# Per-group key, query and probability tiles, and an earlier start of the expert phase, in a fused attention and mixture-of-experts kernel

## The reference, cut to what matters

```
x = x + xattn(layernorm(x), ctx)        # 8 batches, S = 512, D = 256, 16 heads of 16
x = x + moe(layernorm(x))               # 8 experts, HID = 512, the top 2 of each token

xattn: q, k, v projections (k, v from ctx); softmax(q k^T / 4) v; output projection
moe:   gates from softmax(x Wg / 5), top 2, normalised;
       y = sum over the 2 chosen experts e of gate * (gelu(x W1[e] + b1[e]) W2[e] + b2[e])
```

## Time and profile before

| | us |
|---|---|
| time before, median of 3 runs | 816.91 |
| lowest and highest | 812.75, 820.35 |
| the profiled execution, own time | 811.37 |
| its span in the profile | 809.6 |
| last attention product (`pv`) begins | 528.91 |
| first output of the expert phase (`output(0)`) begins | 546.04 |

### The profile page before, as it was taken

How to read it: one execution, slowest core, us unless ns; L and a number is a source line. 1 busy time by engine, 2 the same in 40 slices (tenths; PEclk the granted TensorE clock), 3 DMA queues, 4 the chain that set the end, 5 groups by cost and what they waited for, 6 DMA issues and landing times.

```text
span 809.6 us, 16188 instructions
## 1 busy us (share of the span) xinstructions
PE 751.9 (93%) x4634; PEld 449.7 (56%) x4634; DVE 612.4 (76%) x1123; ACT 455.7 (56%) x663; POOL 393.1 (49%) x354
## 2 busy tenths in 40 slices
PE   7689999999999999999999988759999989999995
PEld 3333434444444444444443433338999879998994
DVE  6586687788788788788788788536786887777674
ACT  1146766766766776776766756744345334444441
POOL 6406125628728728728725604243444455344444
PEclk9669999999999999999999999979999999999998
DMA  5765766757767767757757668874444555454441
GB/s 184 220 164 169 203 171 222 202 184 253 209 196 254 209 191 253 203 182 249 214 169 249 169 161 291 276 241 96 75 94 74 85 128 111 71 79 71 71 74 12
DMA packets 90667, 136.23 MB, mean 168 GB/s; under 512 B 15464, under 2 KB 49224, under 8 KB 90200
## 3 DMA queue, kind: packets, MB, share of 16 engines
q1 hardware_dynamic: 76456, 116.80, 48.0%
q0 software_dynamic: 13296, 17.09, 12.1%
q10 hardware_dynamic: 832, 1.31, 0.5%
HBM read 71.25 MB, written 64.04 MB: 167 GB/s over the span
## 4 chain that ended last, share of the span: by engine, by line
PE 66%; DMA 10%; DVE 10%; issue 5%; ACT 5%; POOL 2%; SPq 1%; POOLq 1%; DVEq 0%; ACTq 0%
PE ps_pv L1521 13%; PE ring L1508 9%; PE ring L1650 8%; PE ring L1668 8%; PE ring L1495 6%; DMA out<-y_sb,xs 6%; PE ps_x L1552 6%; DVE negm L1073 4%; PE ps_x L1570 4%; PE ps_x L1562 3%; ACT probs L1001 3%; PE ring L1659 2%; PE ps_x L1580 2%; PE ps_x L1539 1%; PE ps_pv L1641 1%
## 5 line engine op out<-in xcount | busy, mean ns | idle before, releaser
L1073 DVE TENSOR_REDUCE negm<-ring 128x2 f32<-128x1024 f32 x256 | 310.2, 1222 | 74.7 <-PE ring L1495 72.7
L1001 ACT ACTIVATE probs<-ring 128x1024 f32<-128x1024 f32 x256 | 260.4, 1023 | 91.1 <-PE ring L1508 90.1
L888 POOL DMA_INDIRECT out<-y_sb,xs x71 | 110.2, 1553 | 143.7 <-DMA out<-y_sb,xs 80.7
L1521 PE MATMUL ps_pv<-probs,v_aug 128*32 128x512 f32 x1024 | 139.0, 615 | 5.8 <-ACT probs L1001 5.8
L1508 PE MATMUL ring<-q_st,k_st 64*128 64x512 f32 x512 | 127.9, 499 | 7.0 <-DVE negm L1073 7.0
L1495 PE MATMUL ring<-k_st,q_st 64*128 64x512 f32 x512 | 110.5, 432 | 13.2 <-ACT probs L1001 4.9
L1508 PEld LDWEIGHTS ring<-q_st,k_st 64*128 64x128 f32 x512 | 48.5, 187 | 109.4 <-issue 76.9
L1035 ACT CAST xsT_hi<-ps_pv 128x256 fp32r<-128x256 f32 x71 | 26.4, 372 | 130.8 <-PE ps_pv L1641 130.8
L779 POOL DMA_INDIRECT xs_dram<-xg,rows x64 | 63.4, 991 | 52.7 <-DVEq L1241 32.1
L1668 PE MATMUL ring<-w_hi,hT_hi 128*128 x284 | 85.4, 301 | 0.1
L1668 PE MATMUL ring<-w_lo,hT_hi 128*128 x284 | 80.1, 282 | 0.0
(11 more groups left out here) (189 smaller groups left out, 1205.6 us busy)
## 6 DMA issues: line engine op xcount, KB each, us to landing
k_st<-k_dram SPq DMA_DIRECT2D x64, 192.0 KB
q_st<-q_dram SPq DMA_DIRECT2D x64, 192.0 KB
xs<-xs_dram SPq DMA_DIRECT2D x71, 132.5 KB, 2.4
k_dram<-qk_hi SPq DMA_DIRECT2D x32, 256.0 KB
q_dram<-qk_hi SPq DMA_DIRECT2D x32, 256.0 KB, 2.8
o_dram<-oT SPq DMA_DIRECT2D x32, 256.0 KB, 4.2
w_dram<-w_sb SPq DMA_DIRECT2D x12, 512.0 KB, 4.2
w_hi<-w_dram SPq DMA_DIRECT2D x11, 512.0 KB, 7.3
```

What stands on the lines that cost most here:

```text
L888: pool.indirect_dma_start(out=out, out_offset=bass.IndirectOffsetOnAxis(ap=xs[j % AHEAD][:, TOKEN:TOKEN + 1].bitcast(I32), axis=0), in_=y_ ...
L1001: nc.scalar.activation(probs[:, kt, 2 * jp:2 * jp + 2, :], ring[PLACE["ST", u, p] % RINGS][:], ACT.Exp).then_inc(exp_done, 1)
L1073: nc.vector.tensor_reduce(negm[:, v % 2, :, jp, kt], ring[PLACE["MX", v, p] % RINGS][:], AX.X, ALU.max, negate=True).then_inc(max_free, 1)
L1521: mm = nc.tensor.matmul(ps_pv[2 * DH * j:2 * DH * (j + 1), :], v_aug[:, kt, HPG * g + j, :], probs[:, kt, j, :], start=(kt == 0), stop=(kt ...
```

## The change

What it does:

- `k_st` and `q_st` become four tiles `kq[g]`, one a group, with keys and queries side by side, and `probs` four tiles, one a key tile. They are laid out in an order (kq0, kq1, kq3, probs1, probs0, kq2, probs2, probs3) so that late weights can be loaded over each as it dies. The memsets and the ones rows become four pieces.
- SP's late loads are moved. Into the second and third group of body 7 come `load_b2` (from behind `fetch_o(7, 0)`) and both `load_b1` (from behind the attention phase). The first four `load_rows` come from behind the attention phase to between `put_recip(7, 0)` and `fetch_o(7, 0)`. `load_w2(6)` moves up by one `put_o`. All five `load_w2_hi` (0 to 4; of these 0, 4, 1, 2 were issued by SP in the second to fourth group, 3 by ACT after its last exponential) come behind body 7 in the order 4, 2, 3, 0, 1, each with its own wait, ahead of `put_o(31)`.
- `high_last`: (2,1), (2,4), (3,6) and one after the attention phase become (2,4), (3,1), (3,4) and one after the attention phase; `low_last` follows.
- PE does `turn_x(0)` into `ps_x` before the last `pv`. `hidden(0)` asks for one `low_last` instead of two.
- ACT: `high_xt(0)` ahead of the last `take_o`; then `high_xt(1)` ahead of the last `high_last`.
- DVE: `reciprocals(7, 1)` goes to behind tile 1; `expert_of` stands ahead of `low_xt(1)` and the last `low_last` behind it.

```
-LAST_HIGH = {(2, 1): (2, 5), (2, 4): (1, 7), (3, 6): (2, 6)}
-LAST_LOW = {(2, 4): (2, 5), (2, 6): (1, 7), (3, 7): (2, 6)}
+LAST_HIGH = {(2, 4): (1, 7), (3, 1): (2, 7), (3, 4): (2, 5)}
+LAST_LOW = {(2, 6): (1, 7), (3, 3): (2, 7), (3, 6): (2, 5)}
...
+TAIL_RECIP, TAIL_NORMALISE, ... = 1, 5, ...
...
+            kq, probs = [None] * NG, [None] * NT
+            for kind, n in (("kq", 0), ("kq", 1), ("kq", 3), ("probs", 1), ("probs", 0), ("kq", 2), ("probs", 2), ("probs", 3)):
...
-        ps_xt = ps_pv
+        def ps_xt(j):
+            return ps_pv if j > 0 else ps_x
...
+        def w2_hi_free(eng, e):
+            if e < 2:
+                eng.wait_ge(st_full, NP * G)
+            elif e < 6:
+                eng.wait_ge(pv_done, NT * (G - 1) + (2 if e < 4 else 1))
+            else:
+                eng.wait_ge(st_full, NP * (G - 1))
...
             def load_b1(n):
-                sp.wait_ge(pv_done, NT * (G - 1) + n + 1)
+                sp.wait_ge(st_full, NP * (G - NG + n + 1))
...
                 else:
                     for e in (5, 6):
                         load_w1_hi(e)
+                    load_b2()
                 put_o(NG * i + 1)
                 if not more:
-                    load_w2_hi(1)
+                    for n in range(2):
+                        load_b1(n)
                 if i > 0:
                     store_out(i - 1)
                 put_recip(i, 0)
+                if not more:
+                    sp.wait_ge(tab_done, 1)
+                    sp.wait_ge(scattered, 16 * TOPK * NT * EARLY_B)
+                    for j in range(EARLY_XS + 1):
+                        load_rows(j)
                 fetch_o(i, 0)
...
-                    load_b2()
+                    load_w2(i - 1)
                 put_o(NG * i + 2)
...
+            for e in (4, 2, 3, 0, 1):
+                load_w2_hi(e)
             put_o(G - 1)
...
             high_xt(0)
-            high_last(2, E - 1)
+            take_o(G - 1)
             high_xt(1)
+            high_last(2, E - 2)
             gelu(0)
...
             low_xt(0)
-            low_last(2, E - 1, 4)
-            reciprocals(B - 1, 1)
-            low_xt(1)
             dve.wait_ge(tab_done, 1)
             e = {0: expert_of(0), 1: expert_of(1)}
+            low_xt(1)
+            low_last(2, E - 2, 4)
             dve.wait_ge(b1_in, 32)
...
+            turn_x(0)
+            pv(G - 1, NT - 1)
             pe.wait_ge(tab_done, 1)
             e = {0: expert_of(0), 1: expert_of(1)}
-            turn_x(0)
             pe.wait_ge(w1_hi_in, 16 * (E - 1))
             pe.wait_ge(stage_low, ALL_STAGED)
-            pe.wait_ge(low_done, 2)
+            pe.wait_ge(low_done, 1)
             hidden(0, e[0])
             turn_x(1)
```

More of the change, by code:

```diff
@@ L572, in load_w2_hi, with load_rows @@
             def load_w2_hi(e):
-                sp.wait_ge(st_full, NP * (G - NG + e % NG + 1))
+                w2_hi_free(sp, e)
                 sp.dma_start(w2_hi[:, e].bitcast(F32), w2_dram[e]).then_inc(w2_hi_in, 16)
+            def load_rows(j):
+                if j >= AHEAD:
+                    sp.wait_ge(f_added[j % RING], added_by(j - AHEAD))
+                if j == EARLY_XS:
+                    for g in range(NG):
+                        sp.wait_ge(m_in[g], 16 * B)
+                if j == EARLY_XS + 1:
+                    for n in range(2):
+                        sp.wait_ge(o_stored[n], 16 * G // 2)
+                        sp.wait_ge(den_in[n], 16 * G // 2)
+                row = sp.value_load(row_tab[0:1, j:j + 1], min_val=0, max_val=ROWS - P)
+                sp.dma_start(xs[j % AHEAD][:], xs_dram[bass.ds(row, P), :]).then_inc(xs_in[j % AHEAD], 16)
             def body(i):
@@ L638, in body @@
                 else:
-                    load_b2()
+                    load_w2(i - 1)
                 put_o(NG * i + 2)
-                if not more:
-                    load_w2_hi(2)
                 if i in STAGED:
                     store_stage(i, 1)
-                if i > 0:
+                if 0 < i < B - 1:
                     load_w2(i - 1)
@@ L728, in _ @@
             nc.gpsimd.memset(mhalf[:], -0.5).then_inc(pool_chain, 1)
-            nc.gpsimd.memset(oT[0:1, 0, :], 1.0).then_inc(ones_set, 1)
+            nc.gpsimd.memset(oT[0:2, 0, :], 1.0).then_inc(ones_set, 1)
             nc.gpsimd.memset(pad[:], 0.0).then_inc(ones_set, 1)
-            nc.gpsimd.memset(q_st[:].bitcast(F32), 0.0).then_inc(ones_set, 1)
+            for g in range(NG):
+                nc.gpsimd.memset(kq[g][:, 1].bitcast(F32), 0.0).then_inc(ones_set, 1)
             pool.wait_ge(pool_chain, 2)
@@ L1375, in _ @@
             nc.vector.memset(step[:], 0.0)
-            nc.vector.memset(k_st[:].bitcast(F32), 0.0).then_inc(ones_set, 1)
+            for g in range(NG):
+                nc.vector.memset(kq[g][:, 0].bitcast(F32), 0.0).then_inc(ones_set, 1)
             for part in ("stats0", "stats1", "sums"):
@@ L1426, in tail @@
                 b = B - 1
+                if j == TAIL_RECIP:
+                    reciprocals(b, 1)
                 if j == TAIL_NORMALISE:
```

85 lines of the change are left out of this document (33 added, 52 removed).

## The result

| | before | after | ratio [95%] |
|---|---|---|---|
| median, 20 runs of each | 815.01 | 811.82 | 0.9949 [0.993, 0.9968] |
| lowest and highest | 811.49, 820.35 | 808.55, 815.76 | |
| profiled execution, its span | 811.37, 809.6 | 810.08, 808.4 | |
| a second comparison, beside e1 and e2 (24 and 7 runs) | 808.55 | 803.87 | 0.9927 [0.9901, 0.9954] |
| a third one, beside e7 and e8 (21 and 8 runs) | 809.08 | 803.00 | 0.9939 [0.9912, 0.9966] |

The change takes 0.5% off, 4.2 us of 815 by the ratio, with an interval of 2.6 to 5.7 us. The forecast was 5.2 us and 811.7. The three comparisons give 0.5 to 0.7%, and their intervals overlap. The ratio is not the quotient of the medians: those differ by 3.2, 4.7 and 6.1 us in the three comparisons.

What follows compares the result with a forecast made beforehand. PE was taken as the bound, except 17.1 us before `output(0)` where it mostly waits, chiefly for DVE held by `den`. Order -6.2, clock +0.5, queue +0.5 gave -5.2 us: 816.9 to 811.7, range 807.5 to 817.5.

Steps and rivals of the forecast that it cites:

- The order's -6.2 us: From last `pv` to `output(0)`: without DVE's wait for `den` and with tile 0 earlier, `output(0)` starts 6.2 us earlier.
- fourth rival: First tiles: output additions or a later DVE stage set the pace, little comes through, 815 us; chance 0.05.
- The clock's +0.5: PE around the first hidden layers: granted clock may fall as before, costing 0 to 2 us; +0.5 taken.
- third rival: Low-clock stretches in 507 to 522 and behind the last `pv` both vanish: 7.9 us gained, 809.0; chance 0.15.
- The queue's +0.5: SP's late DMA loads: backlog costs 0 at 356 GB/s, 4.4 us at 289; +0.5 taken, at 330 GB/s.
- (b): `recT` needed for `normalise` at 527.17; its queue ends 524.0 or 527.9 plus some 2 us; delay to 1 us hidden.
- (c): Last `den` lands at 537.4 to 544, tile 4's rows at 540.5 to 547; `turn_x(4)` wants them at 542.7.
- (a): `w2_hi` must be there by 539.8 for `output(0)`; loads end at 536.6 at 356 GB/s, 543.5 at 289.
- first rival: Last `den` and tile 4's rows late at 289 GB/s: gain only 1.8 us, 815.1; chance 0.22.
- second rival: At `turn_x(4)`, queue costs more than the whole gain below 271 GB/s; 818.6 us at 260; chance 0.06.
- Casts, +0.2: Moved casts in the last attention group put the last `pv` 0.2 us later, bounds 0 to +0.6.
- Signs of being wrong: Late `reciprocals(7, 0)`, `normalise(7, 0)` waiting for `recT`, PE waiting for `w2_hi` or tile 4's rows, hidden layer's first matmul 0.79 us.

Runs made afterwards that it cites:

- e1: Kernel before with only the last reciprocals moved behind tile 1 on DVE: 808.62 us, ratio 0.9988 to before.
- e2: Kernel after with the last reciprocals moved back ahead of the first bias addition: 807.88 us, ratio 0.9995 to before.
- e7: Kernel after with e5's edit and the last store of `oT` ahead of two of the five `w2_hi` loads: 804.47 us, ratio 0.9939 to before.
- e8: e7 with both b1 loads behind the first fetch of the third group: 807.53 us, ratio 0.998 to before.
- e4: Kernel after with both b1 loads moved from body 7 to just ahead of the five `w2_hi` loads: 815.02 us, ratio 0.9949 to before.
- before_third: Kernel before, unchanged, traced a third time; median 809.08 us in the third comparison.
- e3: Kernel after with 1 MB of unused DRAM copies behind the five late `w2_hi` loads: 814.03 us, ratio 0.9937 to before.
- e6: Kernel after with tile 0's transposes on PE behind the last `pv` instead of ahead: 814.61 us, ratio 0.9932 to before.
- e5: Kernel after with ACT's last cast and DVE's subtraction of it ahead of tile 1's split: 812.08 us, ratio 0.9921 to before.
- after_again: Kernel after, unchanged, traced a second time; median 803.87 us, ratio 0.9927 to before.
- before_again: Kernel before, unchanged, traced a second time; this execution took 813.29 us, the kernel's median there 808.55.
- after_third: Kernel after, unchanged, traced a third time; median 803.00 us, ratio 0.9939 to before.

## Why the prediction was right, point by point

- **The order's -6.2 us.** Confirmed in the first trace nearly to the tenth: by offsets from the last `pv` the working had `hidden(0)` at +1.5, `hidden(1)` +4.8, `take_h(0)` at +6.3, `hidden(2)` +8.6 and `output(0)` +10.7; the first trace has +1.90, +4.78, `take_h(0)` at +6.35 (539.47), +8.56 and +10.71. Against before's first trace that is -6.4 at `output(0)`, and -5.8 at tile 4 (+14.17 against +20.01), where `hidden(3)` waited 0.30 us for DVE. From tile 4 to the end both took the same (260.7 and 261.1 us), so the fourth rival (little comes through) fell. The two profiled ends still differ by 1.3 us only, since attention ended 4.2 us later in this trace, for which the working had 0.2.
- **What the gain is made of.** The working put `hidden(1)`'s wait down to `den` and moved b1 early without a price for either alone. e2 shows that the `den` move is needed, e1 that it gives nothing measurable alone, and e4 that most of the gain can stay with b1 late. My expectation for e1 had the wait for b1 at the right place (536.8, measured 536.60) and missed by 3 to 4 us in the time: what the trace gives at `output(0)` didn't reach the end, and that stays open.
- **The clock's +0.5.** Measured 0 behind the last `pv`: 1.00 in all three traces of after, 0.73, 0.57 and 0.50 in those of before. Ahead of it the third rival (both low stretches vanish, 7.9 us) came true in two of the three traces of after, where the clock is 1.00 in the last groups too; in the first it is 0.83, lower than before's 0.91, and attention took longer. The sum has no term for this, and it is worth 1.35 us and more in the later pairs. So a part of the gain in the later comparisons is the clock's, above all against before_third, where the wait for `den` was only 1.29 us; the estimate above puts it at about 2 of 5 us.
- **The queue's +0.5.** The term that was mis-sized. In the first trace of after it cost nothing visible, since attention ended at 533. In the other two, with attention ended at 523 to 525, (b) costs 0.6 to 0.9 us (`hidden(0)` at +2.52 and +2.78 instead of +1.90) and (c) 0.72 to 1.16 us, 1.6 to 1.8 together. (a) cost nothing; it does in e4, e7 and e8, where `w2_hi` goes later. This is the first rival, a part of its 4.4 us. With -6.2, clock 0 and queue +1.7 the sum is -4.5; measured are -4.2, -5.9 and -4.9 in the three comparisons. That this agrees is in part luck: the attention phase, which the sum gives 0.2 us, was 4.2 us later in the one pair of traces and 0.5 and 5.1 us earlier in the others. The second rival, the queue costing more than the whole, needed under 271 GB/s (the working counts its 10.8 MB from 506 there and from 507 elsewhere; from 507 it is 278). Over 506 to 540 the three traces of after have 305, 307 and 290; e3 to e6, whose attention phase ended later, have 243 to 272 and didn't lose for it, so the rate over fixed times is a poor measure of it. The working also takes the 7.73 us of `den` as a sign that rows share the engines. They don't show that: `den` stands in SP's own row behind b1, and would wait there either way.
- **Casts, +0.2.** The last `pv` moves by 3 us between traces of the kernel before and by 10 between those of the kernel after, so this was not measurable. e5 shows the order of the last cast to be worth 0.6 us at `output(0)`.
- **`reciprocals(7, 0)`** was forecast at about 515 and came at 516.59, in a trace that ran 2.5 us late by then; the logits, at 520.64, waited for PE and not for it. In after_again it waited 5.01 us for `den` and ended 1.0 us ahead of the logits, which didn't wait.
- **Signs of being wrong** that showed in part: `normalise(7, 0)` waiting for `recT`, PE waiting for tile 4's rows. Neither was large enough to turn the sign.

## What to carry to other kernels

When an engine waits for a transfer, look at what else of the same queue is due within the next microseconds: a wait that is taken away shows the one behind it, and two parts of a change that are worth nothing measurable singly (0.9988, 0.9995) can be worth 0.5 to 0.7% together. Judge such a change by offsets from a common event and by many runs, not by the ends of two profiles, which here differed by 1.3 us where the runs say 4.2. Compare the granted clocks of the two sets of runs as well, since a part of a gain can go with them. Where the DMA engines are busy nearly all the time (0.91 here), expect little of a further reordering: the three tried here (e4, e7, e8) each made another transfer late.

## What was not expected of the hardware

**Pauses of several engines at once.** ACT and DVE of the first trace of after, near 500 us:

```profile
500.26 1.03 ACT L1014 ACTIVATE probs<-ring 128x1024 f32<-128x1024 f32 x1 [3.83 <-remote]
```

```profile
500.31 1.23 DVE L1086 TENSOR_REDUCE negm<-ring 128x2 f32<-128x1024 f32 x1 [1.02 <-remote]
```

The profile puts the release down to "remote", though the kernel uses one core. Of ACT's 3.83 us some 1.7 are idle in the other traces too, and PE stands for 1.02 us only. The same pause (ACT 3.93, 3.93, 4.72, 3.93 us, PE 2.5 to 3.5) stands in the traces of e3 to e6, all from one chip, and in none of before, before_again, before_third, e1, e2, after_again, after_third, e7 and e8. The group in which it falls takes 17.36 us in after and 19.88 to 21.51 in e3 to e6, 15.6 to 15.8 in the others. It is not the only one: the same five traces have up to four more waits of ACT for "remote" of 1.2 to 3.2 us each, near 200, 261, 324, 386 and 448 us and, in e5 and e6, at 547 to 550, and the nine others have none of 0.9 us or more. The window over it in after:

```profile
496.00:501.00 5.00, 3.88 (x22) 1.84 (x14) 1.99 (x3) 1.17 (x2) 3.36 (x4) 1.00 0.94 364
```

The DMA engines are 0.94 busy at 364 GB/s in it, but that is no proof of a cause. No trace of before is known to be from e3's chip, so whether the change brings the pause on some chips, or the chip has it by itself, stays open; a trace of before on e3's chip would tell. The runs on that chip (ratios of 0.9921 to 0.9949) don't show a smaller gain than elsewhere.

**The granted clock differs between executions of the same kernel.** Over 506 to 540 before has 0.85 in one trace and 0.62 in another, with the same instructions, and PE's busy time there goes from 21.46 to 27.14 us. Why it falls so often in one execution and not in another, the traces don't show. With the last `pv` beginning anywhere from 523 to 538 us, it is one reason not to read a difference of a few us off two traces.
